# An LSTM with a residual on one core: twelve plain steps in five banks, x loaded ahead of the weights

## The reference

```python
xW = einsum('ntd,dk->tnk', x, Wx) + b          # x 32x512x512, Wx 512x2048
def step(carry, xw_t):
    prev_h, prev_c = carry
    a = xw_t + prev_h @ Wh                     # Wh 512x2048
    i, f, o = sigmoid of the first, second and third 512 columns of a
    g = tanh(a[:, 1536:])
    next_c = f * prev_c + i * g
    next_h = o * tanh(next_c)
    return (next_h, next_c), next_h
out = x + hs                                   # hs: all next_h, 32x512x512
```

## Time and profile before

| | |
|---|---|
| median of 3 runs | 2535.98 us (2535.93 to 2538.73) |
| profiled execution, time | 2535.94 us |
| profiled execution, span | 2534.1 us |
| PE busy | 2515.8 us, 99% |
| DVE busy | 1983.6 us, 78% |
| ACT busy | 1247.9 us, 49% |
| DMA | 80.21 MB, mean 32 GB/s |

### The profile page before, as it was taken

One profiled execution on the slowest core, in us unless ns is written; L12 is line 12 of the kernel. 1 busy time (PEld: TensorE's weight loads), 2 busy tenths in 40 slices (PEclk: granted clock), 3 DMA queues, 4 the chain that ended last, 5 costly groups with the idle time before them and its releaser, 6 DMA issues.

```text
span 2534.1 us, 155783 instructions
## 1 busy us (share of the span) xinstructions
PE 2515.8 (99%) x67134; PEld 1795.3 (71%) x67134; DVE 1983.6 (78%) x8602; ACT 1247.9 (49%) x5266; POOL 7.2 (0%) x12
## 2 busy tenths in 40 slices
PE   8999999999999999999999999999999999999998
PEld 3577777777777777777777777777777777777775
DVE  7877777777777777777777777777777777777776
ACT  6544444444444444444444444444444444444443
POOL 1000000000000000000000000000000000000000
PEclk9999999999999999999999999999999999999999
DMA  8101101101011011010110110101101001011000
GB/s 234 37 20 30 33 17 33 28 21 33 17 33 33 17 33 25 24 33 17 33 33 17 33 25 25 33 17 33 33 17 33 25 25 33 17 33 33 17 17 18
DMA packets 142169, 80.21 MB, mean 32 GB/s; under 512 B 8620, under 2 KB 139836, under 8 KB 141372
## 3 DMA queue, kind: packets, MB, share of 16 engines
q1 hardware_dynamic: 140548, 75.40, 11.3%
q0 software_dynamic: 1152, 4.19, 0.9%
q10 hardware_dynamic: 440, 0.20, 0.0%
HBM read 42.02 MB, written 33.55 MB: 30 GB/s over the span
## 4 chain that ended last, share of the span: by engine, by line
PE 98%; DVE 1%; DMA 0%; ACT 0%; issue 0%; SPq 0%; DVEq 0%
PE even L327 26%; PE odd L327 26%; PE odd L321 26%; PE even L321 13%; PE s1t_sum L321 6%; DMA w_raw<-in_L_cond_Wx_dram 0%; DVE hw_lo L796 0%; PE odd L340 0%; PE plain_odd L327 0%; PE even L340 0%; PE plain_even L327 0%; PE plain_odd L340 0%; PE plain_even L340 0%; DVE xw_lo L796 0%; DVE f_c L709 0%
## 5 line engine op out<-in xcount | busy, mean ns | idle before, releaser
L709 DVE TENSOR_TENSOR f_c<-i_f,c_state 128x64 f32<-128x64 f32 x1024 | 233.0, 228 | 449.1 <-ACT i_f L561 449.1
L561 ACT ACTIVATE i_f<-odd 128x128 f32<-128x128 f32 x504 | 145.3, 294 | 536.8 <-PE odd L327 536.8
L327 PE MATMUL even<-hw_hi,hT_hi 128*32 128x512 f16 x4032 | 392.1, 379 | 2.4 <-issue 1.9
L327 PE MATMUL odd<-hw_hi,hT_hi 128*32 128x512 f16 x4032 | 392.1, 379 | 1.5 <-DVE hT_hi L658 1.5
L327 PE MATMUL even<-hw_lo,hT_hi 128*32 128x512 f16 x4032 | 392.1, 379 | 0.0
L327 PE MATMUL odd<-hw_lo,hT_hi 128*32 128x512 f16 x4032 | 392.1, 379 | 0.0
L321 PE MATMUL odd<-xw_hi,xT_hi 128*32 128x256 f16 x7936 | 388.6, 273 | 0.0
L321 PE MATMUL odd<-xw_hi,xT_lo 128*32 128x256 f16 x7936 | 388.6, 273 | 0.0
L321 PE MATMUL odd<-xw_lo,xT_hi 128*32 128x256 f16 x7936 | 388.6, 273 | 0.0
L561 ACT ACTIVATE i_f<-even 128x128 f32<-128x128 f32 x504 | 145.3, 294 | 426.1 <-PE even L327 426.1
L571 ACT ACTIVATE tanh_c<-c_state 128x64 f32<-128x64 f32 x1024 | 279.4, 273 | 99.8 <-DVE c_state L719 41.1
(11 more groups left out here) (127 smaller groups left out, 4098.0 us busy)
## 6 DMA issues: line engine op xcount, KB each, us to landing
x_ring<-in_x_dram SPq DMA_DIRECT2D x252, 128.0 KB, 2.8
out_dram<-x_ring SPq DMA_DIRECT2D x252, 128.0 KB
w_raw<-w_raw POOLq DMA_DIRECT2D x8, 512.0 KB, 5.9
w_raw<-in_L_cond_Wx_dram SPq DMA_DIRECT2D x3, 1024.0 KB, 9.4
w_raw<-in_L_cond_Wh_dram SPq DMA_DIRECT2D x3, 1024.0 KB, 15.5
w_raw<-in_L_cond_Wx_dram SPq DMA_DIRECT2D x2, 512.0 KB, 4.5
w_raw<-in_L_cond_Wh_dram SPq DMA_DIRECT2D x2, 512.0 KB, 19.4
x_ring<-in_x_dram SPq DMA_DIRECT2D x6, 64.0 KB, 18.1
```

The costliest lines, as they stand in the source:

```text
L327: mm = nc.tensor.matmul(bank[j * N:(j + 1) * N, :], hT[:, k * N:(k + 1) * N], w[:, k, j, :], start=False, stop=False, skip_group_check=True)
L561: nc.scalar.activation(i_f_half, bank_half, ACT.Sigmoid, scale=UNSCALE).then_inc(if_ready[two], 1)
L709: nc.vector.tensor_tensor(half_of(f_c[:, :], two), half_of(i_f[:, P:2 * P], two), half_of(c_state[:, :], two), ALU.mult)
```

## The change

PLAIN goes from 16 to 12, and the plain steps take their gates in five banks in turn instead of four (the fifth is even[0]). x of steps 4 to 7 is loaded ahead of the weights, half by SP and half by ACT, copied and transposed within the first block of Wx. All low passes of steps 1 to 3 are done before the recurrence of step 0; behind them PE gives a new semaphore, ahead_done. ACT waits for it, then casts x of step 4, h0 (before: DVE), the last quarter of h0 (before: DVE) and Wh. In each pause from step 0 to step 8 PE does ten passes, in that of step 9 the last six. The casts and splits of x for plain steps run five steps ahead instead of four. REST_AT of every formed piece is one step earlier; NEGATE_AT and CAST_AT stay. The loops of ACT and DVE still start at step 16 (UNROLLED), that of PE at step 12. The filling matmuls of `keep_going` come once at the start and in two blocks behind k = 0 and k = 1 of step 0's recurrence, instead of one block behind k = 0, 1 and 2.

```diff
-PLAIN = 16
+PLAIN = 12
-REST_AT = ((5, 5), (6, 6), (7, 7), (8, 8), (9, 9), (10, 10), (11, 11), (12, 12))
+REST_AT = ((4, 4), (5, 5), (6, 6), (7, 7), (8, 8), (9, 9), (10, 10), (11, 11))
+UNROLLED = -(-PLAIN // CHUNK) * CHUNK
+BANKS = 5
 def passes_done(step):
-    return min(34 * step // 3, PASSES * (PLAIN - AHEAD)) if step < 13 else PASSES * (PLAIN - AHEAD)
+    return 10 * (step + 1) if step < PLAIN - 3 else PASSES * (PLAIN - AHEAD)
-        plain_banks = (plain_even, plain_odd, even[1], odd[1])
+        plain_banks = (plain_even, plain_odd, even[1], odd[1], even[0])
...
+        def load_second(engine, j):
+            engine.dma_start(in_ring(j, 0, GROUP, GROUP), x_v[j][:, GROUP:CHUNK, :]).then_inc(x_loaded, 16)
             for j in range(J // 2):
                 load_first(sp, j)
+            for j in range(J // 2):
+                load_second(sp, j)
...
-            for j in range(J):
-                sp.dma_start(in_ring(j, 0, GROUP, GROUP), x_v[j][:, GROUP:CHUNK, :]).then_inc(x_loaded, 16)
...
     # first_step, PE
-                        spread_bias(2, 3)
+                        spread_bias(2, 3, 4)
-                plain_lo(1)
+                pe.wait_ge(xp_ready, AHEAD)
+                for t in range(1, AHEAD):
+                    mm = plain_lo(t)
+                mm.then_inc(ahead_done, 1)
                 pe.wait_ge(hT_lo_ready, 1)
...
-                    keep_going()
+                    if k < J - 2:
+                        keep_going()
+                        keep_going()
...
     # step, PE
-                if plain_steps == PLAIN:
-                    for ahead in range(2, AHEAD):
-                        plain_lo(ahead)
-                elif plain_steps > 0:
+                if plain_steps > 0:
                     plain_passes(passes_done(t - 1), passes_done(t))
...
     # start of ACT
+            for j in range(J // 2, J):
+                load_second(act, j)
...
                     if n == W_B11 and k == 0:
                         cast_plain(0)
+                        act.wait_ge(x_loaded, X_DMA)
+                        act.wait_ge(x_blocks_ready, 2)
+                        copy_x(1)
...
+            act.wait_ge(ahead_done, 1)
+            cast_plain(GROUP)
+            act.wait_ge(h0_loaded, 16)
+            nc.scalar.activation(h_hi[:, :], h0_raw[:, :], ACT.Copy).then_inc(h_hi_ready[0], 1)
+            nc.scalar.activation(h0_last[:, :], h0_raw[...], ACT.Copy, scale=WSCALE).then_inc(h0_last_ready, 1)
             for k in range(J):
                 split_h_hi(k)
...
     # start of DVE
+                    transpose_x(1, 1, 0)
+                    transpose_x(1, 1, 1)
-            dve.wait_ge(h0_loaded, 16)
-            nc.vector.tensor_copy(h_hi[:, :], h0_raw[:, :]).then_inc(h_hi_ready[0], 1)
...
+            rest_plain(GROUP)
             for k in range(J):
                 split_h_lo(k)
```

More of the change, by code:

```diff
@@ L51 @@
 CAST_AT = (3, 4, 5, 6, 7, 8, 9, 10)
-REST_AT = ((5, 5), (6, 6), (7, 7), (8, 8), (9, 9), (10, 10), (11, 11), (12, 12))
+REST_AT = ((4, 4), (5, 5), (6, 6), (7, 7), (8, 8), (9, 9), (10, 10), (11, 11))
 BIAS_AT = 0
+UNROLLED = -(-PLAIN // CHUNK) * CHUNK
 AHEAD = 4
 PASSES = 12
-def passes_done(step):
-    return min(34 * step // 3, PASSES * (PLAIN - AHEAD)) if step < 13 else PASSES * (PLAIN - AHEAD)
+BANKS = 5
 HALVED = (0, 7)
@@ L67, with passes_done @@
 F_EARLY, F_LATE = slice(0, 3), slice(4, 8)
+def passes_done(step):
+    return 10 * (step + 1) if step < PLAIN - 3 else PASSES * (PLAIN - AHEAD)
 def lstm_residual(nc, x, h0, w_x, w_h, bias, out):
@@ L174, in lstm_residual @@
         plain_seeded = sem("plain_seeded")
+        ahead_done = sem("ahead_done")
         early_hi_ready = sem("early_hi_ready")
@@ L331, in plain_bank @@
             def plain_bank(t):
-                return plain_banks[t % AHEAD]
+                return plain_banks[t % BANKS]
             def plain_add(bank, part, halves, w, slot, k):
@@ L339, in plain_add @@
                 for j in range(J):
-                    nc.tensor.matmul(bank[j * N:(j + 1) * N, cols], part[:, slot, k, :], w[:, blocks, k % 2, j, :],
-                                     start=False, stop=False, skip_group_check=True)
+                    mm = nc.tensor.matmul(bank[j * N:(j + 1) * N, cols], part[:, slot, k, :], w[:, blocks, k % 2, j, :],
+                                          start=False, stop=False, skip_group_check=True)
+                return mm
             def spread_bias(*steps):
@@ L355, in plain_lo @@
             def plain_lo(t):
-                pe.wait_ge(xp_ready, t + 1)
                 for k in range(J):
-                    plain_add(plain_bank(t), xp_lo, (0, 1), xw_hi, t, k)
+                    mm = plain_add(plain_bank(t), xp_lo, (0, 1), xw_hi, t, k)
+                return mm
             def plain_passes(first, last):
@@ L364, in plain_passes @@
                     if n % PASSES == 0 or n == first:
-                        pe.wait_ge(plain_seeded, t + 1 - AHEAD)
+                        if t >= BANKS:
+                            pe.wait_ge(plain_seeded, t + 1 - BANKS)
+                        pe.wait_ge(xp_hi_ready, t + 1)
+                    if part == 2 and (k == 0 or n == first):
                         pe.wait_ge(xp_ready, t + 1)
@@ L523, in seed_plain @@
             def seed_plain(t):
-                nc.scalar.activation(plain_banks[t % AHEAD][:, :], bias_scaled[:, :],
+                nc.scalar.activation(plain_banks[t % BANKS][:, :], bias_scaled[:, :],
                                      ACT.Copy).then_inc(plain_seeded, 1)
@@ L535, in cast_plain @@
             def cast_plain(t):
-                act.wait_ge(x_blocks_ready, blocks_count(t // GROUP, 2))
+                act.wait_ge(x_blocks_ready, blocks_count(t // GROUP, 1 + t % 2))
                 first = (A11, A21)[t % 2]
@@ L556, in step @@
                 act.wait_ge(gates_ready, now)
-                bank = plain_banks[t % AHEAD] if plain_steps > 0 else (odd if s % 2 else even)[r % 2]
+                bank = plain_banks[t % BANKS] if plain_steps > 0 else (odd if s % 2 else even)[r % 2]
                 for two in range(2):
@@ L572, in step @@
                                          ACT.Tanh).then_inc(tanh_c_ready[two], 1)
-                if plain_steps > AHEAD:
+                if plain_steps > BANKS:
                     act.wait_ge(o_ready, t + 1)
-                    seed_plain(t + AHEAD)
+                    seed_plain(t + BANKS)
                 if s % 2 == 0 and left >= 3 and plain_steps <= 2:
                     take_s1t1(q + 1)
[L578 to L583, removed]
+                if plain_steps > GROUP + 1:
+                    cast_plain(t + GROUP + 1)
                 if s % 2:
@@ L646, in _ @@
                         cast_plain(t)
+            act.wait_ge(ahead_done, 1)
+            cast_plain(GROUP)
+            act.wait_ge(h0_loaded, 16)
+            nc.scalar.activation(h_hi[:, :], h0_raw[:, :], ACT.Copy).then_inc(h_hi_ready[0], 1)
+            nc.scalar.activation(h0_last[:, :], h0_raw[:, :].rearrange("p (e k) -> p e k", k=J)[:, :, J - 1], ACT.Copy,
+                                 scale=WSCALE).then_inc(h0_last_ready, 1)
             for k in range(J):
                 split_h_hi(k)
-            for t in range(PLAIN):
+            for t in range(UNROLLED):
                 step(t, t % CHUNK, CHUNK, t // CHUNK)
-            steps(mybir.EngineType.Activation, step, begin=PLAIN // CHUNK)
+            steps(mybir.EngineType.Activation, step, begin=UNROLLED // CHUNK)
         @block.vector
@@ L753, in step @@
                         rest_early(q + 3, r + 3)
[L754 to L758, removed]
+                if plain_steps > GROUP + 1:
+                    rest_plain(t + GROUP + 1)
                 if left >= CHUNK:
@@ L840, in _ @@
             transpose_h(h_lo_ready, h_lo, hT_lo, hT_lo_ready, 1)
-            nc.vector.tensor_scalar(out=h0_last[:, :], in0=h0_raw[:, :].rearrange("p (e k) -> p e k", k=J)[:, :, J - 1],
-                                    scalar1=WSCALE, scalar2=None, op0=ALU.mult).then_inc(h0_last_ready, 1)
             dve.wait_ge(h0_last_ready, 1)
             nc.vector.transpose(h0T_last[:, :], h0_last[:, :]).then_inc(h0T_last_ready, 1)
+            rest_plain(GROUP)
             for k in range(J):
@@ L848, in _ @@
             dve.wait_ge(c_zeroed, 1)
-            for t in range(PLAIN):
+            for t in range(UNROLLED):
                 step(t, t % CHUNK, CHUNK, t // CHUNK)
-            steps(mybir.EngineType.DVE, step, begin=PLAIN // CHUNK)
+            steps(mybir.EngineType.DVE, step, begin=UNROLLED // CHUNK)
 _INS = ['x', 'cond_1024', 'L0_cond_Wx', 'L0_cond_Wh', 'L0_cond_b']
```

## The result

The changed kernel takes 2544.29 us in the median of 8 runs (2542.89 to 2545.46), the kernel before 2536.2 (8 runs). The ratio is 1.0028, with a 95% interval of 1.0020 to 1.0037: slower, by 8.1 us. Forecast was 2542.0. The profiled execution has a span of 2542.8 us, 8.7 more than before.

What follows compares the result with a forecast made beforehand. PE, busy 99%, was taken to bound the kernel, with the start bound by arrival, casts and DVE's parts. Start +5.7 and steps 1 to 16 +0.4 gave +6.1: 2535.94 + 6.1 = 2542.0 us; own range 2540.5 to 2543.5, wider 2538.0 to 2545.0.

Steps and rivals of the forecast that it cites:

- rival 1: PE's clock falls in the new holes at the start and before step 12; 2.4 us once, time 2544.4; chance 0.14.
- three signs of being wrong: Wh casts begin by 20 us; PE passes into the loop without a hole; matmul spacing doubles behind a hole.
- The new wait on ACT: At the start, ACT waits for ahead_done before casting h0 and Wh, delaying DVE's sixteen Wh parts; 4.7 us lost.
- f(0): Start of DVE's first operation of step 0, after its sixteen Wh parts; forecast at 35.7 us against 29.97 before.
- x ahead of the weights: At the start, 256 KB loaded first delay the weights 1.0 us; added transposes and copy are absorbed in DVE's gaps.
- Ten passes fit the pause: In the early plain steps, recurrence plus ten passes takes 4.75 us, enough for the gates' chain of 4.67 us.
- r(1): Start of PE's recurrence of step 1; forecast at 37.3 us against 31.60 before.
- S2 and A22: PE waits for DVE's late splits: S2's product starts near 83.8 instead of 82.8; A22 holds PE 3.6 us before the loop.
- The plain steps' saving: Shorter pauses and cheaper last steps between the recurrences of steps 1 and 16 save about 3.9 us.
- DVE's trailing: DVE's fuller queue in steps 4 to 11 makes PE's recurrences later; 0.7 us.

Runs made afterwards that it cites:

- c13: Changed kernel with A22's wait moved behind step 12's recurrence and ACT's ahead_done wait behind its Wh casts: 2532.75 us, ratio 0.9985 to the kernel before.
- a2: Changed kernel with A22's wait kept and five blocks of twelve zero matmuls run on PE ahead of it: 2541.81 us, ratio 1.0019 to the kernel before.
- c13x: c13 with x of steps 4 to 7 loaded behind the weights again, copied behind Wh casts, transposed behind Wh parts: 2532.43 us, ratio 0.9983 to the kernel before.

## Why the prediction was right

The direction and both places were right, and 2544.29 us lies in the range of 2538.0 to 2545.0, which takes in rival 1. The forecast's own range ended at 2543.5, its time was 2.3 us short, and of its three signs of being wrong the third came: the spacing of the matmuls doubled behind a hole (0.43 us for 0.22). What happened is the forecast's mechanism with rival 1 on top, whose time was 2544.4; that it lies so near is in part luck, as the last points show. Point by point:

- **The new wait on ACT** (4.7 us): shown. Moving it gave 4.2 us at f(0).
- **x ahead of the weights** (1.0) and the claim that DVE's transposes and ACT's copy would be absorbed: the step that was mis-sized. DVE's last Wx part ended at 21.1, not 20.0. Its twelve last parts ran from 13.76 without a hole; before it had idled 0.28 and 0.35 us ahead of the last two blocks. There were no gaps left to absorb 1.2 us of transposes, which ACT's wait for the bias (1.25 us) had pushed back as well. The start lost 6.75 in place of 5.7. I had weighed the load's transfer, and not the bias load queued behind two more loads on ACT (7.49 instead of 5.95). That load held PE as well, and ahead_done comes from PE. I had taken PE's last Wx pieces as bound by DVE; in the changed kernel PE has no hole from 7.49 to the end of the last low pass at 25.4 (24.25 forecast), so there its own work set the gate: the late bias, two bias products at half pace (1.68 and 1.71 us instead of 0.86 each), the new block of twelve zero matmuls (1.28 us) and the fifth bank's bias product (0.86 us), none of which the sum had. DVE was as late to within 0.3 us: in c13, where PE was a little earlier, PE waited 0.27 us for the last part. So either alone would have opened the gate about as late; that is argued from these rows, and no run had only one of them.
- **Ten passes fit the pause**: r(1) to r(7) are 38.35, 43.09, 47.84, 52.59, 57.34, 62.09 and 66.94, so 4.75 us apart, and 4.85 at the end, where DVE's step 5 trails, as forecast. r(9) - r(1) was 38.15 us with 38.25 forecast.
- **S2 and A22**: r(11) - r(1) 48.2 (48.1 forecast), the hole ahead of S1's product 0.93 us, the hole ahead of r(12) 3.74 us (3.6 forecast).
- **The plain steps' saving** is real. With both waits out of the way (c13) r(1) to r(16) takes 72.75 us, 3.0 less than before; the sum had 3.9 of savings less 0.7 of DVE's trailing, 3.2. That the version as a whole is 3.9 us faster than the kernel before is another number and agrees by chance: in the spans it is 3.3, the 3.0 less 1.6 for the later r(1), and 1.9 for the exit hole.
- **Rival 1 happened** on top of the forecast rather than in its place. The clock fell with both holes, and in the start DVE covered it, as the rival had it: f(0) followed DVE's sixteen parts directly. At r(12) it cost 2.8 us (a2), with 2.4 as the price in the rival; the slow stretch lasted 5.7 us, longer than the 4.75 that I took as the most. By the warning of the Trainium skill, TensorE: Matmul & The Clock Gate, section Why this matters for your kernels, long idle gaps between bursts lose the full clock; the trace agrees: with the hole of 3.74 us the granted clock fell to 0.50 before PE went on, and behind that of 2.93 us it was 0.50 from 30 to 32 us. Given 0.14, it deserved more.
- **Not seen**: the exit hole's going (-1.6 in the span), which hid part of the above. Forecast and result agree better than their parts do: +1.05 in the start, +0.4 in steps 1 to 11, +2.8 for the clock and -1.6 at the exit make the 2.6 us by which the span's 8.7 passes the 6.1 of the sum.

Two readings of the prediction were off without touching its sum: PE idled 0.65 us or more at three of the four Wx blocks and not at each (at the second it waited 0.04), and from r(1) to r(9) there are eight pauses, not nine (37.3 + 8 x 4.75 is the 75.3 it gives).

The figure of the Trainium skill, DMA: Bandwidth & Descriptors, section Measured (HBM→SBUF), 138 GB/s for transfers of 64 KB (measured there with loads issued from GpSimd), wasn't borne out for these: the last Wx block reached ACT 1.24 us later than before (16.65 against 15.41), and 0.96 later in c13 than in c13x, where 1.0 follows from the row and, as an estimate, 1.9 from the page's figure.

## What to carry to other kernels

A wait costs by where it stands in its queue, not by who reads the data: when a schedule is shortened, look for waits whose margin was steps long (A22's was three), and move each to the first reader. A gate needed by one small operation shouldn't stand ahead of sixteen large ones. A hole in PE can have two prices: its length, and the matmuls at half pace behind it. And before a stretch is put down to the engine that is waited for, look whether the waiting engine had any idle left in it: PE's start had none.

## What the runs showed of the hardware that was not expected

- At the very start the granted-clock column says 1.00 while matmuls go at half pace: eight float32 matmuls take 1.68 us (7.49 to 9.17) in the changed kernel and 0.86 at full pace, in a window (7.4 to 11.0) whose granted clock reads 1.00. Only the spacing shows it there; later the column shows it (0.50).
- The slow stretch behind a hole of 3.74 or 3.75 us varied: the step behind it took 7.66, 6.57 and 7.44 us in three profiled kernels, and 4.89 with the hole filled.
- Work done early can cost: with the bias at 4.11 instead of 7.49 PE idled between pieces, the granted clock was 0.52 from 12.6 to 17.5 us, and PE's projections ended 2 us later.
- A hole of 1.9 to 2.6 us at a loop's exit, put down to "issue", kept its place in the stream of instructions when twelve matmuls were added ahead of it, and was missing in all eight kernels with the shorter straight part.
